# Two-layer graph attention with later graph blocks: look-ups of attention terms that let TensorE mark the candidates of other node tiles, and VectorE take a maximum out of PSUM

## What is computed

```python
feat = (h @ W).reshape(N, H, D)
el = jnp.sum(feat * al, axis=-1)
er = jnp.sum(feat * ar, axis=-1)
e = leaky_relu(el[src] + er[dst], 0.2)
emax = segment_max(e, dst)
ex = exp(e - emax[dst])
a = ex / segment_sum(ex, dst)[dst]
rst = segment_sum(feat[src] * a[:, :, None], dst)
```

## Time and profile before

| | us |
|---|---|
| median of 3 runs | 3291.56 |
| lowest and highest run | 3290.0, 3294.92 |
| the profiled execution: its own time | 3285.96 |
| the profiled execution: its span | 3284.2 |

### The profile page before, as it was taken

One profiled execution on the slowest core, in us unless ns is written; L12 is line 12 of the kernel. 1 busy time (PEld: TensorE's weight loads), 2 busy tenths in 40 slices (PEclk: granted clock), 3 DMA queues, 4 the chain that ended last, 5 costly groups with the idle time before them and its releaser, 6 DMA issues. The chain is left out here.

```text
span 3284.2 us, 78197 instructions
## 1 busy us (share of the span) xinstructions
PE 2195.4 (67%) x11487; PEld 1578.2 (48%) x11488; DVE 2098.1 (64%) x5471; ACT 1409.7 (43%) x4728; POOL 2366.1 (72%) x2399
## 2 busy tenths in 40 slices
PE   6566366777666377767696666686666687666678
PEld 2455355555455255555443444363444465444446
DVE  8899866767599868766784444463444454444446
ACT  2666389989566399988680000030000013000004
POOL 7877767777777767777756777776777763777773
PEclk9799789989899799998897787787887787887778
DMA  5488545444688655443784333353333332333332
GB/s 167 128 228 224 159 141 155 137 142 125 188 228 229 182 152 162 138 142 105 182 287 139 110 110 110 110 144 106 110 110 110 110 99 82 111 110 110 109 108 79
DMA packets 350432, 465.95 MB, mean 142 GB/s; under 512 B 113874, under 2 KB 266557, under 8 KB 346853
## 3 DMA queue, kind: packets, MB, share of 16 engines
q0 software_dynamic: 110992, 281.96, 29.8%
q1 hardware_dynamic: 165948, 113.47, 12.0%
q10 hardware_dynamic: 73116, 67.22, 7.5%
HBM read 385.25 MB, written 76.97 MB: 141 GB/s over the span
## 5 line engine op out<-in xcount | busy, mean ns | idle before, releaser
L455 PE MATMUL t_ps<-t_ring,shared 128*128 x2640 | 912.4, 496 | 478.3 <-ACTq L259 367.0
L455 PEld LDWEIGHTS t_ps<-t_ring,shared 128*128 128x128 f32 x2640 | 592.2, 243 | 789.1 <-issue 706.8
L208 POOL DMA_INDIRECT ring<-feat_d,srcC x770 | 758.9, 986 | 253.6 <-issue 218.6
L208 POOL DMA_INDIRECT t_ring<-feat_d,srcC x754 | 714.9, 948 | 289.1 <-issue 211.1
L290 ACT ACTIVATE ring<-ring,exC 128x64 f32<-128x64 f32 x3128 | 786.0, 335 | 0.0
L455 PE MATMUL bank<-ring,arena 128*128 x1408 | 425.5, 427 | 159.0 <-ACT ring L290 119.6
L373 DVE TENSOR_TENSOR acc<-acc,t_ps 128x256 f32 x440 | 185.4, 421 | 494.3 <-PE t_ps L455 492.7
L678 POOL DMA_INDIRECT attr_d<-abuf,attr_pos x392 | 401.9, 1025 | 117.8 <-issue 117.8
L208 POOL DMA_INDIRECT t_ring<-rel_d,relC x377 | 358.0, 950 | 160.3 <-issue 106.5
L357 DVE TENSOR_SCALAR shared<-lane,dlocT,weightT 128x128 f32<-128x128 f32 x1320 | 406.3, 360 | 50.9 <-PE t_ps L455 29.6
L1904 ACT COPY t_ring<-t_pt 128x512 f32<-128x512 f32 (+1 forms) x14 | 7.8, 554 | 879.0 <-PE t_pt L1871 879.0
(11 more groups left out here) (299 smaller groups left out, 2679.1 us busy)
## 6 DMA issues: line engine op xcount, KB each, us to landing
arena<-lo_d ACTq DMA_DIRECT2D x392, 128.0 KB
t_ring<-feat_d SPq DMA_DIRECT2D x1960, 1.0 KB
t_ring<-feat_d ACTq DMA_DIRECT2D x1624, 1.0 KB
rel_d<-mid_stage SPq DMA_DIRECT2D x25, 1024.0 KB
arena<-attr_d SPq DMA_DIRECT2D x98, 260.0 KB
abuf<-in_attr SPq DMA_DIRECT2D x56, 448.0 KB
ring<-feat_d SPq DMA_DIRECT2D x1536, 1.0 KB
t_ring<-rel_d SPq DMA_DIRECT2D x980, 1.0 KB
```

Source lines behind the costliest of these rows:

```text
L208: pool.indirect_dma_start(out=ring[:, slot_of(u), j, 0:D], out_offset=None, in_=table, in_offset=bass.IndirectOffsetOnAxis(ap=index[:, u, ...
L455: last = pe.matmul(ps[k % len(ps)][:, 0:g.width], hot[:, k % NHOT, j, :], ring[:, slot, j, 0:g.width], start=(j == 0), stop=(j == 1))
```

## The change

Only the look-ups and what feeds them change.

- The candidates of other tiles are no longer masked. The tile numbers of the edges are turned like the places (16 transposes and copies in place of 8) and stored to a second table, `hi_d`. For each group VectorE makes a one-hot of the tile numbers on 64 partitions, 32 for each end. TensorE multiplies it, first of the products of an edge column, with a table that holds 0 at the edge's own tile and -2^120 elsewhere, 228 columns wide, into the same PSUM region; the 6 products with the terms are added on top. A group has 28 products in place of 24.
- VectorE takes the maximum over the 25 candidates straight out of PSUM, in one instruction in place of two, into `found`, with both ends apart. One instruction per layer adds the two ends.
- `make_masks` and `act_masks` are gone; `make_offsets` fills the small table.
- The places are loaded for two groups with one DMA, the tile numbers for six groups with two DMAs on 32 partitions each. One-hots have three buffers in place of two, and the loop has 12 groups in a turn in place of 4.
- POOL waits for the 16 stores of the index tables before its first gather into the ring.

```diff
-    def make_masks(dve):
...
+    def make_offsets(dve):
+        dve.memset(off_tile, 0.0)
+        dve.tensor_scalar(half_part, part[:, :], 32.0, -32.0, ALU.is_ge, ALU.mult)
+        dve.drain()
+        dve.tensor_tensor(half_part, half_part, part[:, :], ALU.add)
+        dve.drain()
         for q in range(2):
+            rows_of = slice(32 * q, 32 * q + 32)
+            dve.tensor_scalar(off_tile[rows_of, P * q:P * q + HEADS * NT].rearrange("p (h n) -> p h n", h=HEADS),
+                              tile_no[rows_of, :].unsqueeze(1).to_broadcast([32, HEADS, NT]),
+                              half_part[rows_of, 0:1], OFFSET, ALU.not_equal, ALU.mult)
...
+        def load_lo(i, kb):
+            act.dma_start(lo[:, kb % 3, :, :], lo_d[:, bass.ds(4 * LAP * i + 8 * kb, 8), :].rearrange("q j p -> q (j p)")
+                          .unsqueeze(0).to_broadcast([P, 2, 8 * P])).then_inc(lo_ready[l][kb % 3], 16)
...
+            if k % 2 and (not static or c + 3 < LOOKS):
+                act.wait_ge(s_src_hot[l], c)
+                act.wait_ge(s_abs[l], c)
+                load_lo(i, (k + 3) // 2)
...
+            dve.wait_ge(hi_ready[l], 64 * i + 32 * (k // HI_GROUPS + 1))
+            dve.tensor_scalar(hi_hot[:, k % 3, :], hi[0:64, k // HI_GROUPS % 2, at:at + 4 * P],
+                              half_part[0:64, 0:1], None, ALU.is_equal).then_inc(s_hi_hot[l], 1)
...
-            dve.tensor_tensor(
-                cand[:, k % 2, :, :, :],
+            dve.wait_ge(s_look[l], c + 4)
+            dve.tensor_reduce(
+                found[:, bass.ds(4 * c, 4), :, :].rearrange("p j q h -> p (j q) h"),
                 pk[k % 2][:, :, :].rearrange("p b (s x) -> p (b s) x", x=P)[:, :, 0:HEADS * NT]
                 .rearrange("p s (h n) -> p s h n", h=HEADS),
...
+                AX.X, ALU.max).then_inc(s_sum[l], 1)
...
             for j in range(4):
+                edges = slice(j * P, (j + 1) * P)
+                goal = pk[k % 2][:, j // 2, 2 * j % 4 * P:2 * j % 4 * P + 2 * P]
+                pe.matmul(goal[:, 0:P + HEADS * NT], hi_hot[:, k % 3, edges], off_tile, start=True, stop=False)
                 for q in range(2):
                     for piece in range(3):
+                        last = pe.matmul(goal[:, q * P:q * P + HEADS * NT], looked[:, k % 3, q, edges],
                                          tab[:, piece, q * HEADS * NT:(q + 1) * HEADS * NT],
+                                         start=False, stop=(q == 1 and piece == 2))
...
     def dve_softmax(dve, l):
         dve.wait_ge(s_sum[l], LOOKS + 2)
+        dve.tensor_tensor(e[:, :, :], found[:, :, 0, :], found[:, :, 1, :], ALU.add)
+        dve.drain()
...
+            pool.wait_ge(s_low, 16 * 16)
             pool.memset(ring[:, :, :, W_GAT - 1:W_GAT], 1.0).then_inc(s_ones, 1)
```

More of the change, by code:

```diff
@@ L1012, in load @@
             for q in range(2):
[L1013 to L1022, removed]
+                act.dma_start(hi[32 * q:32 * q + 32, half % 2, 0:columns * P],
+                              hi_d[q, bass.ds(4 * LAP * i + 4 * HI_GROUPS * half, columns), :].rearrange("j p -> (j p)")
+                              .unsqueeze(0).to_broadcast([32, columns * P])).then_inc(hi_ready[l], 16)
@@ L1025, in group @@
             act.wait_ge(s_look[l], c + 1)
-            act.activation(looked[:, k % 2, 1, :], apart[:, k % 2, :], ACT.Relu, scale=-1.0,
+            act.activation(looked[:, k % 3, 1, :], apart[:, k % 2, :], ACT.Relu, scale=-1.0,
                            bias=ones[:, 0:1]).then_inc(s_dst_hot[l], 1)
         act.sem_inc(s_abs[l], 1)
+        for k in range(5):
+            act.wait_ge(stored[k], 16 * 5 * (l + 1))
         if l:
@@ L1033, in act_look @@
         else:
-            act.wait_ge(s_low, 16 * 8)
+            act.wait_ge(s_low, 16 * 16)
             for k in range(SIGS):
                 act.wait_ge(term_stored[k], TERM_STORES[k])
[L1037 to L1044, removed]
+        load_lo(0, 0)
+        load_hi(0, 0)
+        load_lo(0, 1)
+        with act.Fori(0, LAPS) as i:
+            for k in range(LAP):
+                group(i, k)
+        for c in range(LAPS * LAP, LOOKS):
+            group(*at_look(c))
     def dve_look(dve, l):
@@ L1084, in add_up @@
[L1084 to L1096, removed]
@@ L1097, in dve_look @@
-        for c in range(LOOKS // 4 * 4, LOOKS):
-            pick(c, c % 4)
-            add_up(c, c % 4)
+                AX.X, ALU.max).then_inc(s_sum[l], 1)
+        for c in range(3):
+            one_hots(*at_look(c))
+        with dve.Fori(0, LAPS) as i:
+            for k in range(LAP):
+                pick(i, k)
+                one_hots(i + (k + 3) // LAP, (k + 3) % LAP)
+        for c in range(LAPS * LAP, LOOKS):
+            pick(*at_look(c))
+            if c + 3 < LOOKS:
+                one_hots(*at_look(c + 3))
@@ L1118, in pe_look @@
             pe.wait_ge(s_made, 1)
[L1119 to L1124, removed]
+        pe.sem_inc(s_look[l], 3)
+        with pe.Fori(0, LAPS) as i:
+            for k in range(LAP):
+                group(i, k)
+        for c in range(LAPS * LAP, LOOKS):
+            group(*at_look(c))
     def dve_softmax(dve, l):
         dve.wait_ge(s_sum[l], LOOKS + 2)
+        dve.tensor_tensor(e[:, :, :], found[:, :, 0, :], found[:, :, 1, :], ALU.add)
+        dve.drain()
         dve.scalar_tensor_tensor(out=e[:, :, :], in0=e[:, :, :], scalar=0.2, in1=e[:, :, :],
```

119 lines of the change are left out of this document (67 added, 52 removed).

## The result

| | before | after |
|---|---|---|
| median of 4 runs | 3290.78 us | 3581.92 us |
| lowest and highest | 3286.03, 3294.92 | 3578.47, 3584.11 |
| after / before, 95% interval | | 1.0884 [1.0865, 1.0903] |
| span of the profiled execution | 3284.2 us | 3582.4 us |

A forecast was written before the change was run, and what follows sets the result against it. POOL's list of indirect DMAs was taken as the bound. Waits of 12.1 and 6.9 us removed, plus 2.3 from masks gone, less 3.2 for the new addition, gave 18.1 us saved: 3273 us, range 3262 to 3286.

The forecast's parts named there:

- TensorE's term: Look-ups: 24 products in 1.22 us plus four new ones, 0.46, make 1.68 us a group; 1.75 taken.
- my slots' rule: If ring slots, not POOL, set the end, stage lengthening in both layers reaches the total, less the 9.6 us earlier start.
- the lock between VectorE and POOL: Look-ups: VectorE's two-port modes might stall POOL's descriptor writing; short one-hots were taken to cost POOL nothing.
- The part ahead: Before the look-ups: masks gone, 14.3 us, less 3.4 and 1.3 added; look-ups start 9.6 us earlier, near 149.9.
- VectorE, 1.42 us a group: Look-ups: one maximum from PSUM, 0.9 us, and two one-hots, 0.26 each with rounding.
- ScalarE, 1.50: Look-ups: two activations starting 0.75 us apart, 1.50 us a group; the idle 0.57 before them goes.
- DMA: Look-up loads rise from 256 to 320 KB a group; if transfers hold the stage, 2.2 us a group at worst.
- POOL's chain as the bound: POOL's scatter and gather list sets the block's end; waits of 12.14 and 6.92 us go, total saving 18.1 us.
- the new addition: Behind each look-up stage: adding score halves takes VectorE 1.8 us a layer and holds POOL 1.6 us more.
- (b): Rival: look-ups hardly shorten, from late loads or low clock; 3276 to 3349 us at 2.1 to 2.47 a group; chance 0.10.
- (a): Rival: back-to-back one-hots slow POOL in the look-ups by 0.25 us an instruction, 68 us in all, 3341; chance 0.05.
- (c): Rival: all the saving, 84 us, arrives because consumers, not POOL, set the pace; 3207 us; chance 0.03.

The follow-up runs named there:

- the kernel without holes: The changed kernel with its offset products over all 128 rows instead of 64, zeros in the added rows, one memset a layer added: 3270.77 us, 0.9943 of the kernel before.
- the run of 3411 us: The changed kernel with all 28 look-up products of a group over 64 rows, output not the reference's: 3410.67 us, 1.0363 of the kernel before.

## Why the prediction was wrong, point by point

**The step that failed** is TensorE's term: "4 new ones of 228 columns, which I scale by columns from 100: 0.116 each, 0.46 more, 1.68 us in all", with "the granted clock at 0.97". A group took 3.67 us. Two things were wrong with the term.
- Scaling by columns holds only between products of one height. Each change of height costs 0.11 us, 0.88 us a group. With the clock high throughout that alone would have made 4 x (0.36 + 0.22) = 2.32 us a group, and by my slots' rule 196 x 0.17 - 6 = 27 us more than before, 3318 us (worked out, not run).
- I took the clock of the earlier trace rows for a stage whose products I was changing. At 0.50 a group is 4 x 0.91 = 3.64 us; the other 264 us come from there. The upper bound that I set, 2.47 us "scaled in the same way", had the lower clock in it but no hole; without holes but with all its columns the lower clock measured 4 x 0.69 = 2.76. The 1.79 us of the earlier trace rows was no group at the lower level: the granted clock was 0.50 to 0.51 from 186.96 to 190 and 0.91 from there to 192.3, and a group of 2400 columns takes 2.00 us at 1.2 GHz. The chance of 0.10 for a low clock was too small as well: that the clock was high in the earlier trace rows was seen with another mix of products.

The warning was to be had: the Trainium skill, "TensorEngine Tiling (Array Packing)", section "Key Properties", says that changing the tiling mode drains TensorE. The traces agree, with 0.11 us at each change between 128\*128 and 64\*128; that the clock goes with it is no part of that rule. The prediction weighed the lock between VectorE and POOL instead, which was not where the danger lay.

**The part ahead** was right: the look-ups start at 150.28, forecast 149.9.

**VectorE, 1.42 us a group**, and **ScalarE, 1.50**: in the kernel without holes VectorE is busy 92.43 of 120 us over 60.6 groups of 1.98, 1.52 a group, and ScalarE 1.41; neither is the limit there or in the kernel after.

**DMA**: "at 1.75 ... more than there is" was the sum to follow. Without holes the transfers hold the stage at 1.98 us a group, between my 1.75 and 2.2. ScalarE's queue took 56.7% of the engines for 19.93 MB in 120 us (200 to 320) against 49.2% for 18.80 MB in 150 us: 56.7 x 120 / 19.93 = 341 against 49.2 x 150 / 18.80 = 393, 13% less per byte. The rows are longer there, but no run changed their length alone. The longer period changed nothing, as the saving is the same up to 2.08 us, which the runs bear out (1.79, 1.98 and 2.06 us a group without a wait of POOL).

**POOL's chain as the bound** was right, and so was the size of what it can give: 18.1 us forecast, 18.2 us measured between the medians in the kernel that differs from the changed one in the height and a memset of 2.62 us a layer (3270.77 against 3288.93). That the two agree so closely is partly luck: the interval is 14 to 23 us, and between the profiled executions the end of the second pass moved by 12.3 us. Both waits are gone there. Its passes end where I expected them, give or take a few microseconds: layer 0's last accumulation near 834.6 (forecast 830.5) and layer 1's near 1578.3 (1572.5), in the slowest of its five runs, which is the profiled one. Of its small terms, the new addition costs POOL 7.8 us of longer gathers over the scores where it was 5.7, so 2.1 in layer 0 for my 1.6. The one-hots, which I costed at nothing, cost some: in 160 to 330 us POOL's instructions average 0.961 us where they were 0.950.

**Rivals.** (b) named the clock, in the right direction, but with 3349 us at its worst, since the period was bounded at 2.47. (a) is real and small, 12 us for two spare one-hots. (c) is excluded: 19 us a layer less in the stage gave nothing.

The full-height version beats both kernels, by 0.57% and 8.7%.

## What to carry to other kernels

A product that uses fewer rows is not cheaper for using them: keep all products of a tight sequence at one height, all 128 rows with zeros where needed, or put those of another height together, since every change cost 0.11 to 0.12 us here. (With all of them at 64 rows the holes went too, but the clock stayed at 0.50.) A forecast for TensorE needs the clock of the new mix, not that of the old one; price it at both levels, and if the lower one turns a gain into a loss, that is a case with a real chance. Where an engine's list is the bound, work out how much of a saving has somewhere to go before asking how large it is: here 18 us of some 84.

## What the runs showed of the hardware

- A change between 128-row and 64-row products leaves a hole of 0.11 to 0.12 us, at 1.2 and at 2.4 GHz alike.
- TensorE was busy 100% of a stretch with the granted clock at 0.50, in two forms: full-height work with eight changes in 3.2 to 3.7 us (340 us on end in the kernel after), and half-height work without a hole (240 us on end, 160 to 400, in the run of 3411 us). With four changes a group it was 0.83 to 1.00, with two 1.00.
- The order alone of four spare products moved a kernel from 3590 to 3293 us.
- Rows of zeros in four products of 28 did not keep the clock down: half of the rows of the full-height offsets are zero, and it was 0.97. A stage in which every product has rows of zeros was not run.
- Short one-hots on VectorE cost POOL's indirect DMAs 0.04 us each when four instead of two ran in each group, where one scan of 10.37 us held one of them for its whole length.
